# Writing out the tensor engine's program for 72 routed-expert tiles, with the expert numbers kept

## Chip, cores and metric

One core of one Trainium2 chip. The metric is the device time of one execution in microseconds, lower is better; several executions are made and their median is compared.
## The reference, cut to what matters

Sixteen sequences of 256 tokens with 256 channels go through two blocks, each an attention and a feed-forward part. The change lies in the first feed-forward part, a mixture of experts over the 4096 tokens:

```
scores = softmax(xt @ gate_w.T);  indices = top_k(scores + gate_bias, 2)
combine = one_hot(indices, 8) weighted by scores
for e in range(8):
    y = y + (silu(xt @ w1[e].T) * (xt @ w3[e].T)) @ w2[e].T * combine[:, e:e+1]
z = the same with the shared expert's weights, for every token
```

Inner width is 512. Every token uses two of the eight experts and the shared one.

## The kernel before, in words

The kernel runs in stages that end with a barrier of all engines. First attention, then layer norm statistics, then `moe`: a router (`moe_router`), the shared expert with the routing sums beside it (`moe_shared`), and the routed experts (`mlp_phase`, line 1808, called once with the tag `me`). Then the second attention, which gathers the routed results from memory, and the second feed-forward part.

Routing sorts the 2 x 4096 token-expert pairs by expert into 72 tiles of 128 rows (`SLOT_TILES`, 64 full tiles and 8 for the ragged ends), so each tile belongs to one expert. `IDS` says which token each row is, and `ETAB`, one row of 72 whole numbers in SBUF, which expert each tile has. All weights lie in SBUF as high and low float16 halves (`W1`, `W3`, `W2`), indexed by expert.

For each tile, `mlp_phase` works as follows. POOL copies a column of `IDS` and gathers 128 token rows (`xg`, four buffers). PE turns them by four transposes into `pX` (`xt_transposes`, line 1895), and DVE copies that into `xt`. PE makes six matmuls of 512 columns into `pG` and six into `pU` (`three_products`, line 99: high by high, high by low, low by high). ACT makes silu of `pG` into `SG`, DVE multiplies `SG` by `pU` into `h`. PE transposes `h` in float32 into `pH` (line 1933, four of them), ACT and DVE split that into float16 halves `hh` and `hl`, and PE makes 12 matmuls of 256 columns into `pY` (`down`). DVE copies `pY` into `yb`, SP stores it to `ys`.

The order on PE is written by hand and runs one tile apart: in step `st` PE does the `pX` transposes of tile `st + 1`, `pG` and `pU` of tile `st`, `down` of tile `st - 1`, then the `pH` transposes of tile `st`. All tiles but `xg`, `xt` and `yb` are single buffers. Handover is by semaphores that count tiles, through `Counter.wait` (line 35).

`steps_of` (line 1797) makes the loop: step 0 by itself, a hardware loop (`Fori`) of 17 turns with four steps each (68 steps), and the last three steps by themselves. In the loop the step number is a register, so semaphore values and addresses are worked out by sequencer instructions. DVE has the same loop from `steps_of`; ACT and POOL have a row of shorter loops, with the loads of the next stage's weights between them (`next_load`, `next_high`, `next_low`), and SP has a loop of its own.

`expert(st)` (lines 1898 to 1902) loads the tile's expert number from `ETAB` into a register of PE with `value_load`, and a check of its bounds follows. It is called twice a tile: in `step` ahead of `pG`, and in `down` for the tile before.

Of the kernel before, what the change touches and what calls it, by code (L numbers as in the profile page):

```python
# [91 lines left out]
def three_products(nc, out, a_hi, a_lo, b_hi, b_lo, chunks):  # L92

    n = 0
    last = None
    for kt in range(chunks):
        for a, b in ((a_hi, b_hi), (a_hi, b_lo), (a_lo, b_hi)):
            last = nc.tensor.matmul(out, a(kt), b(kt), start=(n == 0), stop=(n == 3 * chunks - 1))  # L99
            n += 1  # L100
    return last
# [1284 lines left out]
NE, TOPK, F0 = 8, 2, 512  # L1386
# [410 lines left out]
def steps_of(eng, n, step):  # L1797

    step(0, 0, lambda d: d // 4, True, False)  # L1800
    with eng.Fori(0, n // 4 - 1) as i:
        for u in range(1, 5):
            step(i * 4 + u, u % 4, lambda d: i + (u + d) // 4, False, False)
    for st in range(n - 3, n):
        step(st, st % 4, lambda d: (st + d) // 4, False, st == n - 1)

def mlp_phase(nc, ctx, tag, n, W1, W3, W2, consts, routed, ahead):
# [13 lines left out]
    if routed:  # L1822
        IDS, ETAB, rows_d, y_d = routed
# [26 lines left out]
    with nc.Block() as block:  # L1850
        if routed:
            @block.gpsimd
            def _(pool):
                def next_low(j):
                    pool.wait_ge(next_hi, j + 1)
                    nc.gpsimd.tensor_tensor(columns(j, 1), stage[j % 2][:], columns(j, 0), ALU.subtract).then_inc(next_lo, 1)

                def gather(st, q):
                    nc.gpsimd.tensor_copy(idx[q][:], IDS[:, bass.ds(st, 1)]).then_inc(idx_ready.sem, 1)  # L1859
                    idx_ready.wait(pool, st, 1)  # L1860
                    nc.gpsimd.nop(nofuse=True)
                    nc.gpsimd.indirect_dma_start(out=xg[q][:].rearrange("p a d -> p (a d)"), out_offset=None, in_=rows_d,  # L1862
                                                 in_offset=bass.IndirectOffsetOnAxis(ap=idx[q][:], axis=0))\
                        .then_inc(gathered[q].sem, 16)

                for q in range(4):
                    gather(q, q)
                for j, (i0, i1) in enumerate(SPANS):
                    with pool.Fori(i0, i1) as i:
                        for q in range(4):  # L1870
                            xt_full.wait(pool, i * 4, q - 3)
                            gather(i * 4 + q, q)
                    if j < AHEAD:
                        next_low(j)
# [12 lines left out]
        @block.tensor  # L1887
        def _(pe):
            def xt_transposes(st, q, it):

                gathered[q].wait(pe, it, 16)
                xt_ready.wait(pe, st, 0)
                for part in range(2):
                    for kt in range(KD):
                        last = nc.tensor.transpose(pX[:, part, kt, :], xg[q][:, part, kt * P:(kt + 1) * P], ident16[:])
                last.then_inc(xt_full.sem, 1)

            def expert(st):

                if not routed:  # L1900
                    return bass.ds(NE, 1)
                return bass.ds(pe.value_load(ETAB[0:1, bass.ds(st, 1)], min_val=0, max_val=NE - 1), 1)

            def down(st):
                e = expert(st)
                hl_ready.wait(pe, st, 1)
                y_out.wait(pe, st, 0)
                three_products(nc, pY[:], lambda k: hh[:, k, :], lambda k: hl[:, k, :],
                               lambda k: W2[0][:, e, k, :].rearrange("p a n -> p (a n)"),
                               lambda k: W2[1][:, e, k, :].rearrange("p a n -> p (a n)"), FK).then_inc(y_full.sem, 1)  # L1910

            def step(st, q, turn, first, last_one):
                if routed:
                    if first:
                        xt_transposes(0, 0, 0)
                    if not last_one:
                        xt_transposes(st + 1, (q + 1) % 4, turn(1))
                    xt_ready.wait(pe, st, 1)
                    src = xt[q % 2]
                    ah, al = (lambda kt: src[:, 0, kt, :]), (lambda kt: src[:, 1, kt, :])  # L1920
                else:
                    ah, al = (lambda kt: XT[:, 0, kt, bass.ts(st, P)]), (lambda kt: XT[:, 1, kt, bass.ts(st, P)])
                e = expert(st)
                for out, W, full, free in ((pG, W1, gate_full, silu_ready), (pU, W3, up_full, h_ready)):
                    free.wait(pe, st, 0)
                    three_products(nc, out[:], ah, al, lambda kt: W[0][:, e, kt, :].rearrange("p a n -> p (a n)"),
                                   lambda kt: W[1][:, e, kt, :].rearrange("p a n -> p (a n)"), KD).then_inc(full.sem, 1)
                if not first:
                    down(st - 1)
                h_ready.wait(pe, st, 1)  # L1930
                hl_ready.wait(pe, st, 0)
                for k in range(FK):
                    last = nc.tensor.transpose(pH[:, k * P:(k + 1) * P], h[:, k * P:(k + 1) * P], ident[:])  # L1933
                last.then_inc(ht_full.sem, 1)
                if last_one:
                    down(st)
            steps_of(pe, n, step)

        @block.scalar
        def _(act):  # L1940
# [595 lines left out]
```

## Time and profile before

| | us |
|---|---|
| median of 3 executions (2143.4 to 2144.92) | 2144.2 |
| the profiled execution's own time | 2143.76 |
| its span in the profile | 2141.7 |
| time outside the span | 2.06 |

The profile is one execution. Busy shares in it are averages over stages with different limits, so the stage of the change is read by itself: it runs from about 780 to 1126 us of the span. In the chain of waits and in the idle times, "issue" means that the engine waited for nothing that the profile shows, which on PE means that its sequencer had not yet handed it the next instruction.

### The profile page before, as it was taken

To read this page: it belongs to the slowest core of one execution; us is meant where nothing else is said; L and a number is where in the kernel's file an instruction comes from. 1 tells how busy PE (TensorE), PEld (TensorE's weight loads), DVE (VectorE), ACT (ScalarE), POOL (GpSimd) and SP (SyncE) were. 2 spreads that over 40 slices of the span, in tenths; PEclk is the share of its full clock that TensorE was granted. 3 is DMA by queue.
4 is the path that set the end of the run, shared out by engine and by line. 5 is a ranking of instruction groups with operands and counts; after the bars stand their busy time and mean duration, and the time that the engine had idled before them with its cause. 6 is when DMAs were issued, how large, how long until landed. Compare 5 with 4: busy or idle time off the path is not lost. (4 is left out here: it accounts for less than half of the span.)

```text
span 2141.7 us, 45574 instructions
## 1 busy us (share of the span) xinstructions
PE 1743.6 (81%) x14369; PEld 1163.1 (54%) x14375; DVE 1415.4 (66%) x2938; ACT 1103.9 (52%) x2568; POOL 1034.0 (48%) x1543
## 2 busy tenths in 40 slices
PE   0588888886258979999995899999999999998376
PEld 0344444443234546666663676767676767776123
DVE  4356667675975434444444787778787877877796
ACT  1266666664632212222221666666666666666776
POOL 1555555550735732232315666666666666554004
PEclk9689999998569999999997999999999999999697
DMA  3000000000820011222213222222232332320102
GB/s 104 12 9 12 10 10 10 10 5 1 267 78 1 1 47 57 69 71 63 79 44 94 70 73 70 69 72 69 74 78 69 78 77 70 79 63 11 41 1 79
DMA packets 89345, 117.62 MB, mean 55 GB/s; under 512 B 16520, under 2 KB 58768, under 8 KB 89232
## 3 DMA queue, kind: packets, MB, share of 16 engines
q1 hardware_dynamic: 76176, 90.08, 15.6%
q0 software_dynamic: 6528, 17.83, 3.0%
q10 hardware_dynamic: 6528, 8.39, 1.2%
q8 instruction: 47, 0.77, 0.2%
q14 instruction: 66, 0.54, 0.1%
HBM read 56.36 MB, written 17.83 MB: 35 GB/s over the span
## 5 line engine op out<-in xcount | busy, mean ns | idle before, releaser
L1069 POOL TENSOR_SCALAR a_P<-a_P,a_RS 128x256 f32<-128x256 f32 x512 | 254.5, 497 | 235.4 <-DVE a_RS L1351 206.1
L1238 ACT ACTIVATE a_P<-a_pS,a_NM 128x256 f32<-128x256 f32 x512 | 237.9, 471 | 198.3 <-DVE a_NM L1347 194.6
L815 DVE TENSOR_REDUCE a_M<-a_pS 128x2 f32<-128x512 f32 x256 | 164.6, 685 | 142.6 <-PE a_pS L626 142.3
L1247 ACT ACTIVATE a_PH<-a_pT 128x512 f16<-128x512 f32 x256 | 154.1, 602 | 80.5 <-PE a_pT L1163 70.5
L1347 DVE TENSOR_REDUCE a_NM<-a_pS 128x2 f32<-128x512 f32 x256 | 174.7, 682 | 26.3 <-PE a_pS L1155 20.7
L1357 DVE TENSOR_TENSOR a_PL<-a_pT,a_PH 128x512 f16<-128x512 f32 x256 | 172.5, 674 | 16.9 <-ACT a_PH L1247 16.8
L754 ACT ACTIVATE a_PT<-a_pT 128x512 f32<-128x512 f32 x256 | 139.0, 597 | 71.4 <-PE a_pT L645 71.1
L1163 PE MATMUL a_pT<-g_ident,a_P 128*128 128x128 f32 x1024 | 155.9, 275 | 19.9 <-POOL a_P L1069 19.9
L1163 PEld LDWEIGHTS a_pT<-g_ident,a_P 128*128 128x128 f32 x1024 | 120.0, 141 | 38.2 <-POOL a_P L1069 19.3
L1946 ACT ACTIVATE me_hh<-me_pH 128x512 f16<-128x512 f32 x72 | 43.0, 597 | 175.7 <-PE me_pH L1933 175.7
L99 PE MATMUL a_pF<-a_ch,xw_XW 128*128 128x256 f16 x512 | 103.1, 285 | 32.2 <-DVE a_VL L1339 29.2
L1154 PE MATMUL a_pS<-a_KD,a_QS 128*128 128x256 f16 x512 | 126.6, 274 | 0.0
L1155 PE MATMUL a_pS<-a_KZ,a_QS 128*128 128x256 f16 x512 | 126.4, 274 | 0.0
L1991 DVE TENSOR_TENSOR me_h<-me_SG,me_pU 128x512 f32<-128x512 f32 x72 | 49.5, 687 | 98.6 <-PE me_pU L99 98.6
L99 PE MATMUL me_pG<-mo_w1h,me_xt 128*128 x288 | 98.7, 384 | 7.1 <-issue 7.1
L1238 ACT ACTIVATION_READ_ACCUMULATOR a_P<-a_pS,a_NM 128x1 f32 x512 | 102.5, 200 | 0.0
L99 PE MATMUL a_pF<-a_xh,xw_XW 128*128 128x256 f16 x512 | 99.1, 273 | 2.2 <-DVE a_k L1324 1.1
L1151 PE MATMUL a_pS<-a_maskq,g_identb 128*128 128x512 bf16 x256 | 98.1, 383 | 2.0 <-DMA a_QS<-a_QN 1.4
L99 PE MATMUL me_pU<-mo_w3h,me_xt 128*128 x288 | 98.4, 383 | 0.0
L1188 PE MATMUL a_pG<-xw_XW,a_oh 128*128 128x256 f16 x512 | 91.8, 275 | 6.2 <-DVE a_proj L1366 5.3
L1862 POOL DMA_INDIRECT me_xg<-rows,me_idx x72 | 70.4, 977 | 54.8 <-POOL me_idx L1859 52.6
L1944 ACT ACTIVATE me_SG<-me_pG 128x512 f32<-128x512 f32 x72 | 43.0, 597 | 86.9 <-PE me_pG L99 86.9
(442 smaller groups left out, 5251.9 us busy)
## 6 DMA issues: line engine op xcount, KB each, us to landing
a_KD<-a_KN SPq DMA_DIRECT2D x128, 128.0 KB, 2.3
a_QS<-a_QN SPq DMA_DIRECT2D x128, 128.0 KB, 2.3
mr_stage<-mw SPq DMA_DIRECT2D x24, 512.0 KB, 4.7
ys<-me_yb SPq DMA_DIRECT2D x72, 128.0 KB, 1.7
a_ctxin<-ctxT SPq DMA_DIRECT2D x32, 256.0 KB, 2.7
a_KZ<-a_KN SPq DMA_DIRECT2D x64, 128.0 KB, 2.3
g_X<-x SPq DMA_DIRECT2D x1, 4096.0 KB, 15.1
rows<-mr_row ACTq DMA_DIRECT2D x32, 128.0 KB, 3.6
```

The lines of the kernel that those rows point to most:

```text
L99: last = nc.tensor.matmul(out, a(kt), b(kt), start=(n == 0), stop=(n == 3 * chunks - 1))
L754: nc.scalar.activation(PT[(2 * p2 + a) % 8][:], pT[a][:], ACT.Exp, scale=float(dh) ** -0.5).then_inc(p_ready.sem, 1)
L815: nc.vector.reduce_max(M[:, :, a, p2], pS[a][:], AX.X).then_inc(s_max.sem, 1)
L1069: last = nc.gpsimd.tensor_scalar(P32[u % 4][:, a, :], P32[u % 4][:, a, :], RS[u % 4][:, a:a + 1], LIFT, ALU.mult, ALU.mult)
L1151: nc.tensor.matmul(out[:], identb[:], maskq[par][:, j:j + 1, :].broadcast_to([P, 2, S]), start=True, stop=False)
L1154: nc.tensor.matmul(out[:, a, :], q, KD2[par][a][:, p2, :], start=False, stop=False)
L1155: last = nc.tensor.matmul(out[:, a, :], q, KZ[par][a][:, p2, :], start=False, stop=(a == 1))
L1163: last = nc.tensor.transpose(pT[u % 2][:, a, kt, :], P32[u % 4][:, a, kt * P:(kt + 1) * P], ident[:])
L1238: last = nc.scalar.activation(P32[u % 4][:, a, :], pS[u % 2][:, a, :], ACT.Exp, bias=NM[u % 4][:, a:a + 1], accum_out=SM[u % 4][:, a:a + 1])
L1247: nc.scalar.activation(PH[p2 % 2][:, :, :, j * P:(j + 1) * P].rearrange("p a k q -> p (a k) q"), pT[u % 2][:].rearrange("p a k q -> p (a k ...
L1347: nc.vector.tensor_reduce(NM[u % 4][:], pS[u % 2][:], AX.X, ALU.max, negate=True).then_inc(s_max.sem, 1)
L1357: nc.vector.tensor_tensor(PL[p2 % 2][:, :, :, j * P:(j + 1) * P].rearrange(f), pT[u % 2][:].rearrange(f), PH[p2 % 2][:, :, :, j * P:(j + 1 ...
```

## The change

The tensor engine's program of this stage is built by a plain Python loop over the 72 tiles instead of `steps_of`, so it holds no hardware loop and every step number is a constant. `expert(st)` keeps the register that it loaded in a dictionary, so that each tile's number is loaded once; and step `st` calls `expert(st + 1)` behind its `pU` matmuls, ahead of `down(st - 1)`. The programs of the other engines stay as they are. The branch for unrouted tiles in `expert` goes; no call uses it.

```diff
+            chosen = {}
+
             def expert(st):
-
-                if not routed:
-                    return bass.ds(NE, 1)
-                return bass.ds(pe.value_load(ETAB[0:1, bass.ds(st, 1)], min_val=0, max_val=NE - 1), 1)
+                if st not in chosen:
+                    chosen[st] = bass.ds(pe.value_load(ETAB[0:1, st:st + 1], min_val=0, max_val=NE - 1), 1)
+                return chosen[st]
...
                                    lambda kt: W[1][:, e, kt, :].rearrange("p a n -> p (a n)"), KD).then_inc(full.sem, 1)
+                if not last_one:
+                    expert(st + 1)
                 if not first:
                     down(st - 1)
...
-            steps_of(pe, n, step)
+            for st in range(n):
+                step(st, st % 4, lambda d: (st + d) // 4, st == 0, st == n - 1)
```

## Rows read from the trace of the kernel before

**Rows 1.** The page: span, and busy time of each engine over it
```profile
span 2141.7 us, 45574 instructions
PE 1743.6 (81%) x14369; PEld 1163.1 (54%) x14375; DVE 1415.4 (66%) x2938; ACT 1103.9 (52%) x2568; POOL 1034.0 (48%) x1543
```

**Rows 2.** Windows: busy us and counts, PE clock, DMA share, GB/s
```profile
core 0: us, PE busy (x) PEld busy (x) DVE busy (x) ACT busy (x) POOL busy (x), PEclk, DMA share, GB/s
788.00:1122.00 334.00, 327.33 (x2265) 216.74 (x2266) 150.68 (x283) 92.88 (x150) 93.07 (x140) 1.00 0.21 63
```

**Rows 3.** Waits from 788 to 1122 us: total, times, longest
```profile
DVE me_h L1991 <- PE me_pU L99: 98.6, 72, 5.2
POOL me_idx L1859 <- PE me_pX L1895: 66.9, 27, 3.3
ACT me_SG L1944 <- PE me_pG L99: 69.0, 71, 1.6
PEld me_pG L99 <- issue: 9.5, 17, 0.6
PE me_pG L99 <- issue: 6.6, 17, 0.5
```

**Rows 4.** Timeline of PE: start us, us, what
```profile
788.06 0.66 PE L1933 MATMUL me_pH<-g_ident,me_h 128*128 128x128 f32 x4 [0.78 <-DVE me_h L1991]
...
953.40 0.60 PE L1933 MATMUL me_pH<-g_ident,me_h 128*128 128x128 f32 x4
953.84 0.39 PE L1895 MATMUL me_pX<-g_ident,me_xg 128*128 128x128 f16 x4
954.06 0.38 PE L99 MATMUL me_pG<-mo_w1h,me_xt 128*128 x1
...
957.96 0.60 PE L1933 MATMUL me_pH<-g_ident,me_h 128*128 128x128 f32 x4
958.39 0.39 PE L1895 MATMUL me_pX<-g_ident,me_xg 128*128 128x128 f16 x4
959.17 0.39 PE L99 MATMUL me_pG<-mo_w1h,me_xt 128*128 x1 [0.39 <-issue]
...
963.08 0.60 PE L1933 MATMUL me_pH<-g_ident,me_h 128*128 128x128 f32 x4
963.52 0.39 PE L1895 MATMUL me_pX<-g_ident,me_xg 128*128 128x128 f16 x4
963.74 0.38 PE L99 MATMUL me_pG<-mo_w1h,me_xt 128*128 x1
...
1117.99 0.60 PE L1933 MATMUL me_pH<-g_ident,me_h 128*128 128x128 f32 x4
1122.33 0.60 PE L1933 MATMUL me_pH<-g_ident,me_h 128*128 128x128 f32 x4
```

**Rows 5.** Timeline of DVE, the two products `h` beside rows 4
```profile
956.85 0.69 DVE L1991 TENSOR_TENSOR me_h<-me_SG,me_pU 128x512 f32<-128x512 f32 x1 [1.17 <-PE me_pU L99]
961.97 0.69 DVE L1991 TENSOR_TENSOR me_h<-me_SG,me_pU 128x512 f32<-128x512 f32 x1 [1.72 <-PE me_pU L99]
```

**Rows 6.** Sequencer instructions of lines 1801 and 1902, 957 to 959.6 us
```profile
L1801 PEldq ALU_OP  x1: 32/32/32, 957.6 to 957.6; - x1
L1801 PEldq COMPARE_BRANCH  x1: 208/208/208, 957.7 to 957.7; - x1
L1902 PEldq TENSOR_LOAD <-mo_ETAB x1: 298/298/298, 958.3 to 958.3; - x1
L1902 PEldq SEQ_ASSERT  x1: 18/18/18, 958.9 to 958.9; - x1
```

**Rows 7.** The same of lines 35, 1902 and 99, 962.2 to 964 us
```profile
L35 PEldq ALU_OP  x1: 32/32/32, 962.7 to 962.7; - x1
L1902 PEldq TENSOR_LOAD <-mo_ETAB x1: 298/298/298, 962.9 to 962.9; - x1
L99 PEldq FUSED_REGOPS  x1: 46/46/46, 963.6 to 963.6; - x1
```

**Rows 8.** PE's sequencer instructions over the stage: ns minimum/median/maximum
```profile
L1801 PEldq COMPARE_BRANCH  x17: 76/208/227, 806.8 to 1108.5; - x17
L1902 PEldq TENSOR_LOAD <-mo_ETAB x144: 296/307/558, 781.0 to 1122.0; - x144
L99 PEldq ALU_OP  x714: 32/32/36, 789.4 to 1125.3; - x179
L99 PEldq FUSED_REGOPS  x430: 46/46/46, 789.2 to 1125.1; - x144
```

**Rows 9.** The expert load ahead of `down`, 954 to 956.4 us
```profile
L1902 PEldq TENSOR_LOAD <-mo_ETAB x1: 530/530/530, 954.9 to 954.9; - x1
```

**Rows 10.** DMA queues, whole span, then 1205 to 1305 us: packets, MB, share
```profile
q8 instruction: 47, 0.77, 0.2%
...
q8 instruction: 8, 0.13, 0.5%
```

**Rows 11.** PE's weight loads that waited for issue, 1205:1305, then 1400:1500 us
```profile
PEld a_pG L1188 <- issue: 3.6, 14, 0.6
...
PEld a_pG L1188 <- issue: 3.8, 14, 0.8
```

**Rows 12.** Windows of the same two stretches
```profile
1205.00:1305.00 100.00, 93.04 (x825) 71.23 (x823) 80.26 (x191) 64.57 (x203) 62.69 (x96) 1.00 0.30 75
1400.00:1500.00 100.00, 91.51 (x799) 69.61 (x799) 79.15 (x188) 63.73 (x200) 59.67 (x92) 0.98 0.27 67
```

**Rows 13.** The stage's end: timelines of PE, DVE and SP
```profile
1124.43 0.28 PE L99 MATMUL me_pY<-mo_w2h,me_hh 128*128 x1 [1.50 <-DVE me_hl L1995]
...
1125.95 0.42 DVE L1979 COPY me_yb<-me_pY 128x256 f32<-128x256 f32 x1 [1.66 <-PE me_pY L99]
...
1126.54 0.33 SPq L1883 DMA_DIRECT2D ys<-me_yb  x1
```

## The prediction

> **What bounds the kernel now.** I read the page first: PE is the busiest engine, but 81% over the whole span says nothing of this stage [rows 1]. [...]
>
> In the timeline the four `pH` transposes mark the tiles. From 953.40 to 957.96 is 4.56 us, in which PE has no gap at all. From 957.96 to 963.08, a step that opens a new turn of the loop, is 5.12 us, so such a step costs **0.56 us** more [rows 4]. The cause is in the sequencer's own rows. DVE ends `h` at 957.54 (956.85 + 0.69) [rows 5]. The loop's counter is stepped at 957.6 and the branch follows at 957.7 for 0.208 us, although both stand behind the `pH` transposes in the program [rows 6]. So the sequencer had been held at the transposes' wait for `h` and went on only then. It then works out the new step's register values, loads the expert number at 958.3 for 0.298 us, checks its bounds at 958.9, works out the weights' address, and the first `pG` matmul begins at 959.17 [rows 4, 6]. That is 1.63 us after `h`. PE in the meantime has only what is queued: without the gap `pG` would have begun 0.22 us behind the `pX` transposes (as 954.06 behind 953.84), at 958.61, which is 1.07 us after `h` [rows 4, 5]. The sequencer needs 0.56 us more than this cover.
>
> A step within a turn shows how thin the cover is. There `h` ends at 962.66, the load is at 962.9, the address at 963.6 and `pG` at 963.74, 1.08 us after `h`, with no gap on PE [rows 4, 5, 7]. The sequencer arrives just in time; the steps that have a little more register work come a little late, which the sum below picks up.
>
> **The change, part by part.** *The loop goes.* The lost time of the stage is what lies over 4.56 us a tile. From the first `pH` (788.06) to the last (1122.33) are 334.27 us for 71 intervals [rows 4]. The last, 4.34 us, has no `pX` transposes (1117.99 to 1122.33). So 70 x 4.56 + 4.34 = 323.54 us is the stage with PE never late, and **10.7 us** are lost. Of these 17 x 0.56 = 9.5 us belong to the turns; the other 1.2 us are the entry and small delays of a few hundredths.
>
> *Registers become constants.* Semaphore values and the index into `ETAB` need no instructions any more. What stays is the address work from the expert number: 714 and 430 instructions of 32 and 46 ns behind line 99 over the stage [rows 8], placed between matmuls where it is hidden now (the steps of 4.56 us hold it). I take its cost as nothing; if the cover were gone it would be the thin margin of the step within a turn over again, at most the few hundredths of the 1.2 us.
>
> *One load of the expert number goes, the other moves.* Now there are 144 loads of 307 ns in the median [rows 8], two a tile. The one ahead of `pG` lies on the path just described, with its check and register work some 0.7 us (962.9 to 963.6) [rows 7]; it disappears from there. From `h` to `pG` the sequencer then needs about 1.0 - 0.7 = 0.3 us against a cover of 1.07, so it is early by about 0.75 us. The new load stands behind `pU`, exactly where `down` has its own now: at 954.9 for 0.530 us, with PE working on `pG` since 954.06 and busy without a gap until 957.96 [rows 4, 9]. There is still one load at this place. Its price is nothing, and if the cover were gone 0.31 to 0.56 us a tile [rows 8]. Queued behind it are only `down` and the `pH` transposes of the same PE; DVE's copy of `pY` waits for those.
>
> *What is late next.* With the sequencer early, PE is back to back. The other engines keep their programs; each would have to lose its idle time before PE noticed. DVE waits for `pU` 98.6 us, and ACT 69.0 us for `pG` [rows 3]. The `pH` transposes start at 957.96 and `h` is ready at 957.54, so that wait has 0.42 us to spare even in a step of 4.56 us [rows 4, 5]. POOL waits for `pX` 66.9 us [rows 3], so the gathers are ahead. These are the same margins as in today's steps without a gap; the change makes no step shorter than those.
>
> *The end of the stage* follows PE: last `down` at 1124.43, waiting for `hl`, then the copy at 1125.95 and SP's store at 1126.54 [rows 13]. All of it moves forward with PE, and so does the barrier.
>
> *Written-out code must be fetched.* The stage has 32 matmuls and as many weight loads a tile, and about 20 sequencer instructions: 1144 / 72 = 16 behind line 99 [rows 8], one load, one check, two or so waits. That is about 84 a tile. [...] The nearest row speaks for nothing: 1205 to 1305 us is written-out code with a fetch every 12 us, 1400 to 1500 us is the loop of the same attention, and the issue ahead of its `pG` is 3.6 us in 14 waits in the one and 3.8 us in 14 in the other [rows 11]; PE is busy 93.04 and 91.51 us [rows 12]. I take 0, and keep a part of the upper end for the range.
>
> **Sum.** 2143.76 - 10.7 = 2133.1 us for an execution like the profiled one. The median of the runs lies 0.4 us above it (2144.2), so the prediction is **2133.5 us**, 0.5% faster.
>
> [...]
>
> **The rivals.** *A, the forecast*: the sequencer is early, 10.7 us go. For it: the step of 4.56 us has all the work but the turn [rows 4].
>
> *B, only part of it goes.* The sequencer stays close behind, for instance because waits that were joined to register instructions become instructions of their own, so that each tile keeps a delay of some hundredths. With 0.05 us in each of 71 tiles, 3.6 us stay: 2137.1. Against it: about 0.7 us a tile leave the path.
>
> *C, only the branch instruction goes.* If the late issue came from the work on the new tile rather than from the turn, the saving would be the branch alone, 17 x 0.21 = 3.5 us [rows 8]: 2140.7. Against it: the load that makes up half of that work goes too.
>
> *D, slower: fetching the code.* Place: each 16 KB boundary of PE's program. PE stops when the next packet hasn't come by the time its queue is used up. With each packet's 1.0 us exposed, 26 - 10.7 = 15.3 us are lost: 2159.5. It decides from 10.7 / 26 = 0.41 us exposed at each packet. Against it: rows 11, where eight packets added nothing that can be seen. For it: no row shows this stage's code in a row, nor 72 tiles of it.
>
> *E, the clock.* PE would be busy almost without a pause. If the granted clock fell by 3% for the stage, 0.03 x 323 = 9.7 us come back: 2143.2, no change. Against it: 1.00 at 98% busy now [rows 2].
>
> **How the numbers follow.** Chances: A 0.84, B 0.08, C 0.02, D 0.03, E 0.03. A by itself has 1.5 us to either side, since the clock's rise at the start of the next stage can fall a little earlier or later in its work, and the runs shown spread by 1.5 us. The range, **2131.0 to 2137.5**, takes A and B. A measurement of this kernel can tell 0.2% from no change, 4.3 us, so faster means under 2139.9: A and B and a piece of D where little of a fetch is exposed, 0.93; same is C and E, 0.05; slower the rest of D, 0.02.
>
> **What would show it.** In the profile of the changed kernel: `pH` transposes 4.56 us apart at every tile; no "issue" idle ahead of `pG`, against 17 now; 72 loads from `ETAB` instead of 144, none of them between `pX` and `pG`; no compare-and-branch of PE in the stage; about 26 more packets on q8; first to last `pH` near 323.5 us; stages after it the same length. The prediction is wrong if `pH` intervals stay over 4.6 us (B), if PE idles for issue at places some 14 us apart, beside q8 packets (D), or if the clock in the window is under 1.00 (E).

## The result and the profile after

The changed kernel takes 2136.81 us in the median of 8 runs (2131.24 to 2140.3); eight runs of the kernel before give 2144.56. The ratio is 0.9956, with a 95% interval from 0.9937 to 0.9974: **0.44% faster**, 9.4 us. (The ratio is not that of the two medians, which are 7.8 us apart; it lies at that of the means, 2136.4 and 2146.0.) Forecast were 0.50% and 2133.5 us, with a range of 2131.0 to 2137.5. The profiled execution took 2135.91 us, its span is 2134.0 us, 7.7 us under that of [rows 1].

First the stage itself. Windows of the changed kernel: the routed stage, then the second attention.

```profile
788.00:1111.00 323.00, 323.00 (x2265) 212.86 (x2264) 150.72 (x282) 92.58 (x150) 93.18 (x140) 1.00 0.22 66
1117.00:1965.00 848.00, 762.79 (x6608) 580.05 (x6609) 649.85 (x1533) 525.98 (x1635) 507.38 (x773) 0.97 0.29 71
```

PE is now busy for all of the 323.00 us, with the 2265 matmuls for which it needed 334 us in [rows 2], at the same clock of 1.00. The timeline of PE, the first, two middle and the two last `pH` groups:

```profile
787.45 0.66 PE L1936 MATMUL me_pH<-g_ident,me_h 128*128 128x128 f32 x4 [0.78 <-DVE me_h L1995]
...
956.23 0.60 PE L1936 MATMUL me_pH<-g_ident,me_h 128*128 128x128 f32 x4
...
960.79 0.60 PE L1936 MATMUL me_pH<-g_ident,me_h 128*128 128x128 f32 x4
...
1106.70 0.60 PE L1936 MATMUL me_pH<-g_ident,me_h 128*128 128x128 f32 x4
1111.04 0.60 PE L1936 MATMUL me_pH<-g_ident,me_h 128*128 128x128 f32 x4
```

First to last are 323.59 us; forecast was 323.54. Every interval is 4.56 us, give or take 0.01, but the first (4.62) and the last (4.34). The sequencer's rows and DVE's `h` show why (first DVE, then the sequencer's waits, its address work for `pG`, and the one load):

```profile
955.12 0.69 DVE L1995 TENSOR_TENSOR me_h<-me_SG,me_pU 128x512 f32<-128x512 f32 x1 [1.16 <-PE me_pU L99]
```

```profile
L35 PEldq EVENT_SEMAPHORE  x2: 51/51/51, 955.9 to 956.0; - x2
...
L99 PEldq FUSED_REGOPS  x1: 46/46/46, 956.1 to 956.1; - x1
...
L1902 PEldq TENSOR_LOAD <-mo_ETAB x1: 303/303/303, 957.1 to 957.1; - x1
```

`h` is ready at 955.81. The sequencer goes on at once and has the address of the next `pG` at 956.1, some 0.3 us after `h`. In the kernel before, that address came 1.6 us after `h` in a step that opens a turn (the `pG` matmul behind it at 1.63 us [rows 4, 5]) and some 1.0 us after it within a turn [rows 5, 7]. The load of the next expert number comes at 957.1, while PE works on `pG` and `pU`. There are 72 loads in all.

The surprise is behind the stage. The second attention has a hardware loop of its own on PE, closed by the branch at line 966. Its branches and the instruction fetches on q8, before:

```profile
L966 PEldq COMPARE_BRANCH  x6: 76/208/211, 1317.6 to 1830.9; - x6
```

and after:

```profile
L966 PEldq COMPARE_BRANCH  x6: 82/3769/4150, 1306.0 to 1822.2; - x6
...
q8 instruction: 113, 1.85, 0.4%
```

Five taken branches of **3.7 to 4.2 us** stand where there were five of 0.2, and q8 moved 113 packets instead of 47. The windowed DMA view puts 24 of them into the stage (3 before), and 45 between 1305 and 1820 us, the turns of that loop, where the kernel before has none. So code is fetched at each turn of a loop for which none was fetched before: 9 packets of 16 KB a turn (45 in five) against none. Between its first and its last branch the loop took 516.2 us instead of 513.3. The ends of the stages tell what of the gain was kept: the first `pG` matmul of the attention (line 1081) begins at 1126.35 instead of 1137.93, 11.6 us earlier; its last (line 1188) at 1966.18 instead of 1974.71, 8.5 us earlier. The experiments tell whether the 3 us between the two come from the long branches.

### The profile page after: what moved, and what is told of

The parts are those of the page before. It is cut to its first block and busy times, and to the rows that moved or that the text cites. A ratio compares the mean times of both kernels' runs of the same rounds, so it can differ in the third digit from the quotient of the medians.

```text
span 2134.0 us, 45257 instructions
## 1 busy us (share of the span) xinstructions
PE 1750.5 (82%) x14369; PEld 1163.1 (55%) x14374; DVE 1412.6 (66%) x2938; ACT 1105.4 (52%) x2568; POOL 1036.7 (49%) x1543
## 5 line engine op out<-in xcount | busy, mean ns | idle before, releaser
L1331 DVE SCALAR_TENSOR_TENSOR a_QN<-a_pF,a_bqk,a_QN 128x256 f16<-128x256 f32 x128 | 55.9, 479 | 48.7 <-ACT a_QN L1221 45.0
```

## The experiments

Every packet on q8 has 16,384 bytes in these traces. In the built programs the one before has 12,053 instructions on PE, and q8 moved 47 packets, so an instruction has about 64 bytes (47 x 16,384 / 12,053 = 63.9, an estimate that takes all of the packets for PE's program) and a block of one packet 256 slots. The head of PE's loop in the second attention could be put on a chosen slot of such a block. The loop has 1,760 instructions, 6.9 blocks: from slots 0 to 32 it lies in 7 blocks, from any later slot in 8. The change puts 5,539 instructions ahead of it, 21 blocks and 163 slots, so a head that was on slots 0 to 32 comes to 163 to 195. All medians stand beside runs of the kernel before on the same chip.

### The change once more, and with the loop put right

`as_changed` is the changed kernel. `unrolled_fit` adds, for PE alone:

```diff
-        with eng.Fori(0, B // 2 - 2) as i:
+        if eng is nc.tensor:
+            loop = nc.Fori(0, B // 2 - 2, engines=[nc.tensor.engine], head_slot={nc.tensor.engine: 0})
+        else:
+            loop = eng.Fori(0, B // 2 - 2)
+        with loop as i:
```

> The changed kernel once more, beside the others on one chip. In its first profile the routed stage has pH transposes every 4.56 us (787.45 to 1111.04 us), 11.3 us gained to the stage's end, but the back branch of PE's loop in the second attention (line 966) takes 3.7 to 4.2 us in five turns where it took 0.21 before, and q8 moved 113 packets instead of 47. Theory: the longer program shifted that loop over one more 16 KB block than PE's instruction memory keeps, so its code is fetched again at every turn; some 3 us of the gain are given back there. Expected: 0.4% faster than before, 113 packets, five long branches. Rival (the long branches are chance, or come from other traffic at that moment): they vary from execution to execution, and 113 is not repeated.

> The change as it is, and the head of PE's loop in the second attention put on the first slot of a 16 KB fetch block; nothing else. Theory: the loop's 6.9 blocks then lie in 7 blocks instead of 8, the five branches take 0.21 us again, q8 falls from 113 to about 69 packets, and the time is about 3 us under the changed kernel as it is, near 2133.5 us (0.5% under before), with less scatter. Rival (the program's whole length, or its traffic, makes the branches long): 113 packets and five branches of 3.8 us stay, and the time does not move.

`as_changed`: 2135.84 us against 2145.68, ratio 0.9947 [0.9928, 0.9967]; 113 packets and five branches of 3.4 to 4.1 us again. `unrolled_fit`: 2131.67 us, ratio 0.9934 [0.9916, 0.9953]. Its branches and packets:

```profile
L970 PEldq COMPARE_BRANCH  x7: 76/208/311, 1204.3 to 1818.9; - x7
...
q8 instruction: 69, 1.13, 0.2%
```

Seven branches are listed, since `head_slot` puts one more ahead of the loop, at 1204.3 us; it took 0.3 us. The long branches and 44 packets went with the place of the loop alone; the rival of the longer program falls. What stays, 69 - 47 = 22 packets, is the written-out code. The intervals of the two ratios overlap, so the 3 us were not shown by this.

### The loop put wrong in the kernel before

`loop_misfit` is the kernel before with `head_slot` 128 in the same place.

> The kernel before, with the head of PE's loop in the second attention put on slot 128 of a fetch block, so that the loop spans 8 blocks; the routed stage untouched. Theory: the long branches and some 45 more q8 packets (about 92) appear without the change, and the kernel is about 3 us slower than before (2147.5), the routed stage the same. Rival (they belong to the longer program): 47 packets, branches of 0.21 us, no change.

```profile
L970 PEldq COMPARE_BRANCH  x7: 83/3757/3960, 1213.3 to 1827.2; - x7
...
q8 instruction: 92, 1.51, 0.3%
```

92 packets and five long branches (3.7 to 4.0 us), as forecast, without any of the change. With `unrolled_fit` this shows that the place of this loop's head decides whether the loop is fetched again: no packet in its five turns with the head on slot 0, 45 with it on slot 128. That the kernel before has its head on slots 0 to 32 is worked out from its missing packets and not seen directly. But the time: 2143.9 us in the median of 12 runs, ratio 0.9991 [0.9977, 1.0006]. **No cost can be seen**; 3 us more were expected. The cause of the long branches was right and their price too high.

The timeline shows where the stop goes. PE in the changed kernel around its first long branch (1306.0 us):

```profile
1306.52 0.60 PE L1163 MATMUL a_pT<-g_ident,a_P 128*128 128x128 f32 x4
...
1310.16 0.65 PE L1163 MATMUL a_pT<-g_ident,a_P 128*128 128x128 f32 x4 [2.39 <-POOL a_P L1069]
```

and in the kernel before around its own (1317.6 us):

```profile
1318.23 0.60 PE L1163 MATMUL a_pT<-g_ident,a_P 128*128 128x128 f32 x4
...
1320.98 0.65 PE L1163 MATMUL a_pT<-g_ident,a_P 128*128 128x128 f32 x4 [1.51 <-POOL a_P L1069]
```

From one group to the next it is 3.64 us against 2.75. PE had queued work for a part of the 3.8 us and would have waited 1.51 us for POOL anyway, so 0.9 us is left at this place in this turn, and PE, busy some 92% of this loop [rows 12], has room to make it up. The profiles say that it does: from the first to the last branch of the loop are 516.2, 513.4, 513.9 and 512.9 us with the stops (`after`, `as_changed`, `as_changed_2`, `loop_misfit`) and 511.1 to 513.8 us in six profiles without them (`before`, both of `unrolled_fit`, both of `loop_one_load`, `unrolled_two_loads`). The 3 us of the first profile came once and not again.

### The other half alone: the loop kept, one load a tile ahead

`loop_one_load` keeps the hardware loop and loads into four registers in turn, without a bounds check at either place; `step` takes the register ahead of the `pX` transposes; attention's head on slot 0.

```diff
+            kept = [pe.alloc_register(f"expert{q}") for q in range(4)]
+            def load_expert(st, q):
+                pe.reg_load(kept[q % 4], ETAB[0:1, bass.ds(st, 1)])
+            def expert(q):
+                return bass.ds(pe.snap(kept[q % 4], min_val=0, max_val=NE - 1), 1)
...
+                if not last_one:
+                    load_expert(st + 1, q + 1)
                 if not first:
-                    down(st - 1)
+                    down(st - 1, q - 1)
```

> The other half of the change by itself: the hardware loop of the routed stage stays, but each expert number is loaded once, a tile ahead, into one of four registers that are used in turn (the bounds check goes with it); the attention's loop head is on slot 0. Theory: what made the turns late is the sum of register work after h, 1.63 us against a cover of 1.07; without the load, its check and their register work (0.65 us) it is 1.0, so that steps that open a turn come out at 4.56 to 4.6 us too, the stage gains 10 us or more, and the time is near 2134, with about 47 q8 packets. Rival (the turn by itself costs the 0.56 us): 5.1 us at every fourth pH interval stays, the stage gains 1 to 2 us, time near 2143.

2135.28 us, ratio 0.9944 [0.9924, 0.9965]. Timeline of PE:

```profile
951.15 0.60 PE L1943 MATMUL me_pH<-g_ident,me_h 128*128 128x128 f32 x4
...
955.71 0.60 PE L1943 MATMUL me_pH<-g_ident,me_h 128*128 128x128 f32 x4
...
960.27 0.60 PE L1943 MATMUL me_pH<-g_ident,me_h 128*128 128x128 f32 x4
...
964.83 0.60 PE L1943 MATMUL me_pH<-g_ident,me_h 128*128 128x128 f32 x4
...
969.39 0.60 PE L1943 MATMUL me_pH<-g_ident,me_h 128*128 128x128 f32 x4
```

Five groups span a whole turn, with 4.56 us each time; no 5.12 is left. First to last `pH` are 323.59 us (791.49 to 1115.08), what the written-out program has, with 48 packets. In the turn at 955 us `h` is ready at 955.29, the branch comes at 955.4, and the address of the next `pG` at 956.0: 0.7 us after `h` instead of 1.6. The turn was not the cause by itself. (The branch that `head_slot` puts ahead of the attention's loop took 3.7 us in this profile, once.)

### The first half alone: written out, two loads a tile

`unrolled_two_loads` is the change without its dictionary and without `expert(st + 1)`; attention's head on slot 0.

> Only the loop written out: the expert number is loaded twice a tile at the old places, once between the pX transposes and pG and once in down; attention's loop head on slot 0. Theory: in a step within a turn the sequencer needed 1.0 us after h against a cover of 1.07, and without the turn's and the waits' register work every step is such a one or better, so pH intervals are 4.56 us throughout and the stage gains the same 10.7 us: either half of the change is enough. Rival (the load on the path is what was late): intervals of 4.6 us and more stay, the stage gains some 9 us or less.

2137.21 us against 2146.69, ratio 0.9956 [0.994, 0.9971]. Its `pH` groups, with 144 loads:

```profile
953.67 0.60 PE L1934 MATMUL me_pH<-g_ident,me_h 128*128 128x128 f32 x4
...
958.23 0.60 PE L1934 MATMUL me_pH<-g_ident,me_h 128*128 128x128 f32 x4
...
962.79 0.60 PE L1934 MATMUL me_pH<-g_ident,me_h 128*128 128x128 f32 x4
```

4.56 us again; 65 of the 71 intervals are this, the first is 4.83 and one 4.69, and first to last are 323.97 us, 0.4 us more than with the whole change. So either half of the change is enough to within 0.4 us; with one in place the other brings next to nothing.

### Measuring the margin

`unrolled_plus2` puts two idle loads with their checks back on the path (below), `loop_plus1` one (always of tile 0's number) into the kernel before, both with the attention's head on slot 0:

```diff
                 e = expert(st)
+                for _ in range(2):
+                    pe.value_load(ETAB[0:1, st:st + 1], min_val=0, max_val=NE - 1)
```

> The change (attention's loop head on slot 0) with two more loads of an expert number, each with its bounds check, put back between the pX transposes and pG of every tile; nothing uses them. It measures the margin. Theory (the sequencer is held at the pH transposes until h is ready, and has 1.07 us from there to pG): the changed kernel needs about 0.3 us of it, each load with its check 0.65, so two make 1.6 us, and pH intervals become about 5.1 us, 38 us in all, time near 2171. Rival (the sequencer runs a whole tile ahead, and its work counts only in sum): 27 sequencer instructions a tile leave room in 4.56 us, intervals stay 4.56 and the time stays near 2133.

> The kernel before (attention's loop head on slot 0) with one more load of an expert number and its check ahead of pG of every tile. Theory: steps within a turn have 0.1 us of margin left, so they grow by about 0.55 us to 5.1, steps that open a turn by the full 0.65 to 5.8; 71 of them make some 40 us, time near 2185. Rival (sequencer work counts only in sum): intervals within a turn stay at 4.56.

`unrolled_plus2`: 2169.8 us (forecast 2171), ratio 1.0104 [1.0062, 1.0145]. `loop_plus1`: 2191.75 us (forecast 2185), ratio 1.0206 [1.0166, 1.0246]. Each is the median of two runs. The `pH` groups of the first, then of the second, where the third interval shown opens a turn:

```profile
951.37 0.60 PE L1942 MATMUL me_pH<-g_ident,me_h 128*128 128x128 f32 x4
...
956.44 0.60 PE L1942 MATMUL me_pH<-g_ident,me_h 128*128 128x128 f32 x4
```

```profile
949.88 0.60 PE L1939 MATMUL me_pH<-g_ident,me_h 128*128 128x128 f32 x4
...
955.19 0.60 PE L1939 MATMUL me_pH<-g_ident,me_h 128*128 128x128 f32 x4
...
960.39 0.60 PE L1939 MATMUL me_pH<-g_ident,me_h 128*128 128x128 f32 x4
...
966.19 0.60 PE L1939 MATMUL me_pH<-g_ident,me_h 128*128 128x128 f32 x4
```

5.07 us against a forecast of 5.1 (over the stage 5.05 to 5.23 but for its ends, 5.11 in the mean); and 5.31, 5.20 and 5.80 us against 5.1 and 5.8. Between the stalls PE's sequencer has plenty of time, and still each load counts in full once the cover is used up. That is what a sequencer held at the wait for `h` does, and not one that runs a tile ahead. A step within a turn lost 0.1 to 0.2 us more than forecast, so its margin before was nearer to nothing than to 0.1 us. Another 1.7 us of the 6.8 that `loop_plus1` lies over its forecast are in the very first interval, 7.56 us where 5.20 + 0.65 were to be expected: the matmuls of its `pG` and `pU` took 0.63 us instead of 0.38, and the granted clock from 790 to 792.6 us was 0.51 (1.00 from 792.6 to 796 us).

### What the misplaced loop costs

> The changed kernel again beside the next two, to settle what the misplaced attention loop costs in time. So far its second attention took 848.1 and 846.0 us between barriers with five branches of 3.5 to 4.2 us, against 844.6 to 845.7 us with branches of 0.2; but the kernel before with the loop misplaced took 844.7. Theory now: the stop of 3.8 us at each turn falls where PE waits some 2 us for DVE and POOL anyway and is made up by its spare time later in the turn, so that 1 us or less of it is left in the whole time. Rival: 3 us are left, 0.14%. Expected: 113 packets, 0.5% faster than before, within 1 us of unrolled_fit_2 by the theory, 3 us over it by the rival.

> The change with the attention's loop head on slot 0, again. 69 packets, branches of 0.2 us. By the theory within 1 us of as_changed_2, by the rival 3 us under it.

> The hardware loop kept, each expert number loaded once and a tile ahead, attention's loop head on slot 0, again. Its stage had the same 323.59 us from first to last pH as the changed kernel, with 48 packets instead of 113. Expected: the same time as unrolled_fit_2 within 1 us, since neither has anything left to gain in the stage; 0.5% under before.

Against 2145.37 us before: `as_changed_2` 2137.55 (12 runs), ratio 0.9965 [0.9948, 0.9982]; `unrolled_fit_2` 2135.46 (10 runs), 0.9956 [0.9939, 0.9974]; `loop_one_load_2` 2130.78 (7 runs), 0.9936 [0.9913, 0.9959]. The 2.1 us between the first two lie between the theory's 1 and the rival's 3. Over all runs of each kernel the means are 2135.7 (29 runs, standard error 0.8) for the change, 2133.8 (16 runs, 0.9) for `unrolled_fit` and 2132.4 (13 runs, 1.1) for `loop_one_load`. So the misplaced loop costs **1.9 us, give or take 2.4** (two standard errors): it stays open whether it costs anything. `loop_one_load_2` was forecast within 1 us of `unrolled_fit_2` and came out 4.7 us under it; over all runs the two kernels are 1.4 us apart, give or take 2.9, so no difference is shown. Whichever is faster, the hardware loop with one load a tile has all of the stage's gain with one packet more than the kernel before.

## Why the prediction was right, and where it was not

*What bounds the stage.* Right. PE set the pace before, busy 327.33 of 334.00 us at a granted clock of 1.00, with DVE next at 150.68 [rows 2], and it waited for issue ahead of `pG` 17 times, as many as the loop has turns [rows 3]. PE's sequencer, held until `h` and then 0.56 us longer than the queued work lasts at each turn, was the only loss. The sum of 10.7 us is 10.68 in the trace (334.27 - 323.59), and the two kernels with added loads lose what this reading says, within 0.2 us a tile.

*The loop goes; one load goes.* The parts were priced together, and their sum is right. The split of the 10.7 us, 9.5 to the turns, describes where the time was seen, not what caused it: removing the load with its check from this path alone recovers all of it. Of the other 1.2 us most are 0.05 to 0.12 us in one further step of each turn. The turn's work and the load's were terms of one sum, 1.63 us against 1.07, and taking either brings it under the cover. Rival C, the branch alone for 3.5 us, is ruled out in the stage by `loop_one_load`, which keeps the branch and has the whole gain.

*Registers to constants, the moved load, what is late next.* Each priced at nothing, and nothing was seen: PE has no gap from 788 to 1111 us.

*Rival B* (some hundredths stay in each tile): no tile keeps any. *Rival E* (the clock falls in the stage): the granted clock is 1.00 from 788 to 1111 us.

*Written-out code.* In the stage the exposed cost was taken as nothing, and that is right: 24 packets, no wait. The count of this code's packets was sized a little too high: the program grew by 5,539 instructions (5,400 were estimated), but they came as 22 packets, not 26, which is 65 bytes an instruction (22 x 16,384 / 5,539) and not 80. The 80 came from a stretch with a packet at either end (8 packets for 7 blocks), and the sequencer's own instructions in it were not counted.

**What the prediction missed** is behind the stage. "About 26 more packets" was wrong, since there are 66 more, and "stages after it the same length" left their loops out of the reckoning. Rival D looked for fetches at the boundaries of the new code, where they are hidden (24 packets in the stage, and PE busy 323.00 of 323.00 us); the fetches that stop PE, 3.7 to 4.2 us at a branch, are at the back branch of a loop that the change doesn't touch, because 21.6 more blocks ahead of it moved its head within a block. Whether the forecast of the length failed too stays open: the attention grew by 3.1 us in the first profile (11.6 - 8.5), which no other profile repeats, and by the repeated runs the stops cost 1.9 us, not clear of nothing. That the missed stops did not spoil the forecast was luck: as far as the runs show, they fell where PE waits anyway (1.51 us for POOL in the kernel before).

*The distance that is left.* 2133.5 was forecast and 2136.8 measured. All 29 runs of the change have a mean of 2135.7 and all 63 of the kernel before 2145.7, so the change gains 10.0 us, give or take 1.8, and 10.7 were forecast. Part of the distance is the starting point: the three runs known ahead had a median of 2144.2, 1.5 us under that mean.

What the runs show of this loop: in 7 blocks it was kept, with no packet in its five turns and a branch back of 0.208 us (`before`, `unrolled_fit`); in 8 blocks it was fetched with 9 packets a turn, and the branch took 3.7 to 4.0 us (`loop_misfit`). Why the packets are nine where the loop lies in eight blocks is not shown.

## What to carry to other kernels

Look at what the sequencer does between the last wait that holds it and the next instruction of a busy engine: that stretch, not the sum of its work, has to fit under the queued work, and one term taken out of it can be worth as much as all of them. Before writing a loop out, try to move its slow register load (307 ns in the median here [rows 8]) away from that stretch; it gave the same in this stage without a longer program. What can be taken out is worth no more than the lateness: here 0.56 us a turn, though the path became 1.3 us shorter (1.6 to 0.3). When a program grows, look at the back branches of the loops behind it and at the packets on q8; where they tell of a loop that is fetched at each turn, its head can be placed. Here, with a loop of 6.9 blocks of 16 KB, that saved five stops of 3.8 us, and no gain in time could be shown: at this place PE waits 1.51 us for POOL anyway.

## What the runs showed that was not expected

The back branch of PE's loop in the second attention took 0.21 to 0.23 us in the profiles with no packet on q8 at its turns, and 3.3 to 4.2 us in every turn of the four profiles with 9 packets a turn (45 in five turns). With the stop, PE's granted clock falls at another place. Windows of the changed kernel right behind its second, third and fourth long branch:

```profile
1412.00:1417.00 5.00, 3.69 (x25) 2.40 (x26) 2.93 (x9) 2.30 (x8) 2.17 (x4) 0.73 0.16 52
1515.00:1521.00 6.00, 4.75 (x30) 3.03 (x31) 3.19 (x10) 3.15 (x10) 2.17 (x4) 0.72 0.12 41
1618.00:1625.00 7.00, 5.35 (x28) 3.40 (x29) 2.95 (x10) 3.09 (x10) 2.13 (x4) 0.58 0.11 34
```

and of the kernel before at the same places of its loop:

```profile
1423.00:1428.00 5.00, 3.88 (x33) 2.69 (x34) 3.79 (x11) 2.76 (x10) 2.60 (x5) 1.00 0.17 54
1526.00:1532.00 6.00, 4.67 (x39) 3.29 (x40) 4.36 (x12) 3.56 (x12) 2.92 (x6) 1.00 0.15 50
1628.00:1635.00 7.00, 5.85 (x46) 3.94 (x47) 5.11 (x14) 4.35 (x15) 3.58 (x7) 1.00 0.14 40
```

The granted clock there is 0.58 to 0.73, a mixture of 0.50 and 1.00, the only two values in the clock records of these profiles, where it was 1.00 in the kernel before, and fewer matmuls fit into the same time, 28 against 46 in the last pair. Ahead of it PE had been idle for 2.2, 2.2 and 2.6 us, where the kernel before has 1.5 us each time. But the kernel before has such falls in this loop too, only later in the turn, some 15 us behind the branch and behind another wait:

```profile
1333.00:1337.00 4.00, 4.00 (x23) 3.00 (x21) 3.28 (x9) 1.58 (x6) 2.16 (x4) 0.57 0.11 33
1640.00:1645.00 5.00, 4.06 (x23) 2.94 (x24) 4.16 (x9) 2.42 (x8) 2.19 (x5) 0.66 0.09 28
```

In the four profiles with the stops, 14 of the 20 turns have a fall within 6 us of the start of the branch by the traces' clock records; in the six without them none has. The time at the lower level over the loop is 20.4, 13.6, 13.6 and 10.2 us with the stops and 3.4 to 10.2 us without, so part of the falls are moved and part may be added; that they cost time is not shown, as the length of the loop above says.
